# Last attention: VectorE's products for the weighted edges in pieces of 512 columns instead of 1024

## What is computed

```
h = (x @ W_att).reshape(n, H, D)                    # H = 8, D = 64
e = leaky_relu(a_src[src] + a_dst[dst], 0.2)
e = exp(e - segment_max(e, dst)[dst])
s = segment_sum(e, dst)
alpha = e / (s[dst] + 1e-16)
out = segment_sum(alpha[:, :, None] * h[src], dst)
att_out = out.mean(axis=1) + bias_att
```

## Time and profile before

| | |
|---|---|
| time, median of 3 runs | 5556.75 us (5547.52, 5556.75, 5561.84) |
| the profiled execution | 5550.81 us, of which its span is 5549.0 us |
| busy, whole span | DVE 73%, POOL 65%, PE 45%, ACT 23% |
| chain that ended last, by engine | POOL 52%, issue 20%, DVE 15%, PE 9% |
| chain that ended last, largest line | POOL, L789 (both attentions' gathers): 36% |
| gathers of the last attention (L789) | 864, from 4167.1 to 5300.7 us |
| L1848, whole run | 216 instructions of 1024 columns, 265.8 us |

### The profile page before, as it was taken

The page is one execution under the profiler, slowest core; times in us unless marked ns, Lnnn a source line. Parts: engine busy times, 40 slices in busy tenths (PEclk is TensorE's granted clock), DMA queues, the critical chain, the costliest instruction groups (busy, mean ns, idle before and its releaser), DMA issues.

```text
span 5549.0 us, 51316 instructions
## 1 busy us (share of the span) xinstructions
PE 2490.4 (45%) x13082; PEld 1703.0 (31%) x13082; DVE 4026.8 (73%) x7062; ACT 1267.1 (23%) x4430; POOL 3599.8 (65%) x3763
## 2 busy tenths in 40 slices
PE   1697100101121143423333344479864677677644
PEld 0571000001121132323232234457751233233224
DVE  9877888887886687878787878545543676776756
ACT  0000000000000011111111111110004777777741
POOL 2777777777777777777777777410017777777730
PEclk6555555555555555555555555589977888888876
DMA  6222111111222223232222223247741222222230
GB/s 250 56 55 57 48 55 48 55 61 51 53 52 71 54 80 82 80 82 80 81 81 82 78 76 98 73 152 255 236 126 46 79 91 78 79 87 82 76 101 13
DMA packets 392369, 477.20 MB, mean 86 GB/s; under 512 B 216403, under 2 KB 252309, under 8 KB 384966
## 3 DMA queue, kind: packets, MB, share of 16 engines
q1 hardware_dynamic: 136550, 279.94, 15.0%
q0 software_dynamic: 114832, 133.36, 10.5%
q10 hardware_dynamic: 140752, 61.28, 3.9%
HBM read 295.04 MB, written 179.24 MB: 85 GB/s over the span
## 4 chain that ended last, share of the span: by engine, by line
POOL 52%; issue 20%; DVE 15%; PE 9%; DMA 3%; ACT 0%; POOLq 0%; DVEq 0%; ACTq 0%; SPq 0%
POOL arena L789 36%; POOL rec_dram L746 13%; PE acc L2186 3%; DVE OHX L1515 3%; PE pw L2174 2%; DVE oh L1525 1%; DVE arena L1537 1%; DVE V L1557 1%; DVE arena L1541 1%; POOL own_dram L766 1%; DVE sc L1542 1%; PE acc L1993 1%; DVE oh L1515 1%; PE acc L2128 1%; POOL arena L819 1%
## 5 line engine op out<-in xcount | busy, mean ns | idle before, releaser
L789 POOL DMA_INDIRECT arena<-tab_dram,jst x2592 | 2521.5, 973 | 778.2 <-issue 773.0
L746 POOL DMA_INDIRECT rec_dram<-V,rowst x784 | 837.5, 1068 | 232.0 <-issue 225.3
L2120 PE MATMUL pw<-OHX 128*128 128x128 bf16 x1632 | 209.5, 309 | 789.7 <-DVE OHX L1515 788.4
L2128 PE MATMUL acc<-arena,oh 128*128 128x64 f32 x1952 | 428.6, 421 | 253.5 <-DVE oh L1525 253.5
L2128 PEld LDWEIGHTS acc<-arena,oh 128*128 128x128 f32 x1952 | 418.7, 331 | 267.8 <-issue 267.8
L970 ACT ACTIVATE arena<-arena,ew 128x64 f32<-128x64 f32 x1728 | 417.8, 333 | 34.4 <-PE acc L2220 34.4
L2220 PE MATMUL acc<-OHX,ident 128*128 128x512 f32 x432 | 254.7, 755 | 369.9 <-ACT OHX L970 369.9
L970 ACT ACTIVATE OHX<-arena,ew 128x64 f32<-128x64 f32 x1728 | 417.8, 333 | 2.5
L2120 PEld LDWEIGHTS pw<-OHX 128*128 128x128 bf16 x1632 | 156.0, 140 | 840.9 <-DVE OHX L1515 840.9
L1537 DVE TENSOR_TENSOR arena<-arena,pt 128x1024 f32<-128x1024 f32 x108 | 131.8, 1221 | 382.7 <-DMA arena<-tab_dram,jst 380.6
L739 POOL TENSOR_TENSOR pdum<-pdum 128x1 f32<-128x1 f32 x197 | 53.2, 270 | 449.7 <-DVE arena L1812 198.3
(11 more groups left out here) (566 smaller groups left out, 6244.8 us busy)
## 6 DMA issues: line engine op xcount, KB each, us to landing
arena<-tab_dram,jst POOLq DMA_INDIRECT x2592
arena<-rec_dram SPq DMA_DIRECT2D x122, 288.0 KB, 3.7
mt_dram<-oh ACTq DMA_DIRECT2D x272, 128.0 KB, 1.7
rows_dram<-V SPq DMA_DIRECT2D x27, 1056.0 KB, 4.0
rows_dram<-arena SPq DMA_DIRECT2D x27, 1056.0 KB, 4.3
V<-in_edge_attr_dram ACTq DMA_DIRECT2D x97, 256.0 KB
oh<-mt_dram SPq DMA_DIRECT2D x42, 512.0 KB, 4.7
OHX<-mt_dram SPq DMA_DIRECT2D x38, 512.0 KB, 4.7
```

Of the source, the lines that this page charges most:

```text
L746: gp.indirect_dma_start(rec[:, :], bass.IndirectOffsetOnAxis(ap=rowst[:, q, k:k + 1], axis=0), recst[:, q, k, :], None).then_inc(S[f"scat{ ...
L789: gp.indirect_dma_start(hd.G[:, a.r, j, :], None, table[:, :], row_of(jst[:, a.r, j:j + 1])).then_inc(S[f"rows{a.r}"], 16)
L2120: last = nc.tensor.matmul(unit_bank(c.slot)[:, k // 2 * P:(k // 2 + 1) * P], mones[c.slot][:, 0, k, :], mones[c.slot][:, 1, k, :], start=k ...
L2128: last = nc.tensor.matmul(o, roh[:, c.q, k, :], RG[:, c.r, k, 0:D], start=False, stop=True, skip_group_check=True)
```

## The change

VectorE's products of a step are made one edge at a time: four instructions of 512 columns instead of two of 1024, with the same inputs, outputs and places. Each of the first three raises the chain's semaphore and is waited for, where before only the first one was. The count of steps in a block's chain goes from 22 to 30 (2 more in each of 4 steps). Nothing else is changed: no DMA, buffer or other engine's instruction is added or moved.

```diff
             def weighted3(a, f, st):
 
                 slot_taken3(v, a, f)
-                for k in range(0, 8 - VA, 2):
+                for k in range(8 - VA):
                     t = f * 8 + k
-                    ins = V.tensor_tensor(V3r[vslot[f]][:, k * 512:(k + 2) * 512].rearrange("p (k h d) -> p k h d", h=H3, d=D),
-                                          G3[:, a.r, t:t + 2, 0:D].unsqueeze(2).to_broadcast([P, 2, H3, D]),
-                                          ew[:, a.q, t * H3:(t + 2) * H3].rearrange("p (k h) -> p k h", h=H3).unsqueeze(3)
-                                          .to_broadcast([P, 2, H3, D]), ALU.mult)
-                    if k + 2 < 8 - VA:
+                    ins = V.tensor_tensor(V3r[vslot[f]][:, k * 512:(k + 1) * 512].rearrange("p (h d) -> p h d", d=D),
+                                          G3[:, a.r, t, 0:D].unsqueeze(1).to_broadcast([P, H3, D]),
+                                          ew[:, a.q, t * H3:(t + 1) * H3].unsqueeze(2).to_broadcast([P, H3, D]), ALU.mult)
+                    if k + 1 < 8 - VA:
                         st(ins)
                     else:
                         ins.then_inc(S["dvd"], 1)
 
             def block3(a, c):
 
                 if a:
-                    st = Steps(v, "dc", 22, a.g)
+                    st = Steps(v, "dc", 30, a.g)
...
-                assert not a or st.k == 22, st.k
+                assert not a or st.k == 30, st.k
```

## The result

The changed kernel takes 5577.3 us (median of 5 runs, 5576.0 to 5581.2); the kernel before took 5555.2 in five runs beside them (5547.5 to 5561.8). The ratio is 1.0044, with a 95% interval from 1.0029 to 1.0058: slower by 22 us. Predicted were 5577 us, and slower. The profiled execution of the changed kernel took 5581.2 us, 5579.4 of it span.

A forecast was written before the change was run, and what follows sets the result against it. The last attention's time was taken as the sum of POOL's gathers. Added waits, 16 x 1.05 - 5 x 0.1 + 5 x 1.2 = +22 us, taken as 23, on a 5554 us base gave 5577 us; range 5562 to 5590.

The forecast's parts named there:

- POOL sets the stage: Last attention: its time is the sum of 864 gathers, 868.8 us busy, 53.2 of them waiting on VectorE's instructions.
- Length of a piece: L1848 with 512 columns: 0.692 us, taken from L1944's same shape; half a 1024-column instruction, 0.613, was the lower bound.
- Cover: VectorE's added 1.5 us a block costs nothing, hidden by waits on TensorE (2.3 us) and ahead of L1865 (9.0).
- The sum: Added gather waits over 26 blocks of the last attention: +22 us, 23 carried gather by gather.
- 16 common blocks: Gather blocks beside VectorE work like its block 13: each waits +1.05 us more.
- five first of a loop turn: Blocks where VectorE stands 0.43 us later ahead of its first products: waits change by -0.1 us each.
- five at the ends: Blocks at the two ends, whose first three product groups each meet a gather already: +1.2 us each.
- step 3: A block's last products, started by TensorE at any phase against gathers: waits 0.44 to 0.38 us, taken as 0.
- Rival 1: Gathers let through miss the next piece, so L1848's 43 us of waits become 22: 5533 us, chance 0.06.
- Rival 2: Gathers meet all product groups at any phase and L1831's waits stay: -4 us, 5550 us, chance 0.10.
- Rival 3: Idle time ahead of L1865 is gone, so VectorE's added work costs 42 us: 5596 us, chance 0.03.
- Rival 4: Each piece could stand 0.94 us behind a gather on the shared port: +165 us, 5719 us, chance 0.01.

The follow-up runs named there:

- runs 1: Kernel before, pairs kept, with a 352-column fill of an unused tensor on VectorE behind the products of a block's first three steps: 5593.9 us, stage 1171.7.
- run 7: Kernel before, VectorE's product pairs replaced by constant fills of 1024 columns that read nothing: 5568.8 us, stage 1150.4 where 1116 was expected.
- run 5: Changed kernel, but a piece does not wait for the one ahead of it: 5538.0 us, stage 1129.4.
- run 9: Changed kernel, pieces and waits kept, with a single-element sum ahead of the products of a block's first three steps: 5551.8 us, stage 1136.1.

## Why the prediction was right, step by step

- *POOL sets the stage, and a wait inside a gather moves all that follows.* Held: busy of L789 +24.4, stage +24.5, tail unchanged. In every run the stage is 1080.5 us and the waiting, within 0.2: 161.5 of waiting gave 1242.2, 22.6 gave 1103.0. Of the ten stages that were forecast ahead of their runs with a number, eight came within some 6 us; runs 1 and 7 missed by 16 and 34, both with a fill that starts late.
- *Length of a piece, 0.692 taken between 0.613 and 0.692.* Measured 0.693. The row of another line with the same shape was the right one to take. A piece and its wait took 0.726, as worked out.
- *Cover.* Held as named: steps 0 to 2 in the wait on TensorE, the rest ahead of the scores. The idle time there did not shrink by 1.5 us a block as the prediction's bound allowed, it grew by 0.6.
- *The sum.* Forecast were +1.05, -0.1 and +1.2 us for a block of each kind. Counted over all: 16 common blocks +1.17, five first of a loop turn +0.06, five at the ends +1.05; 18.7 + 0.3 + 5.3 = 24.3 us, against 22 by hand and 23 by replay. For the common block, term by term (measured: the 15 behind the first, which by themselves gained 1.20):

| | forecast | measured |
|---|---|---|
| step 0 | 0 to 0.28 | 0 to 0.28 |
| step 1 | 0.86 to 0.63 | 0.87 to 0.67 |
| L1831 behind it | 0.05 to 0.77 | 0.05 to 0.78 |
| step 2 | 0 to 0.28 | 0 to 0.28 |
| step 3 | 0.44 to 0.38, taken as 0 | 0.40 to 0.51 |

- *Where terms were off.* In the first blocks of a loop turn step 1 was to fall from 1.01 to 0.28, and step 2 to rise to 0.28; they came to 0.68 and 0.12. Two errors, +0.40 and -0.16, and step 3 fell there by 0.10; five blocks of 27 made them small. The step that failed is that VectorE stands 0.43 us later there. It did before, and not after: step 0 began 9.49 us behind the start of the scores before (9.05 to 9.08 in all common blocks but one), and 9.14 after. The time went from the idle stretch ahead of the first L1834, in the timeline before and after in the same block:

```profile
4886.94 0.69 DVE L1834 TENSOR_TENSOR V<-V,acc 128x512 f32<-128x512 f32 x1 [0.49 <-DVE V L1832]
```
```profile
4908.91 0.69 DVE L1834 TENSOR_TENSOR V<-V,acc 128x512 f32<-128x512 f32 x1
```

It is 0.49 us before and 0.13 after; why it got shorter stays open. Step 3, too, isn't at any phase, as the prediction had it: its wait goes by the block's place in the loop turn (before, from block 10 on: 0.94 to 0.97 us in the second, 0.27 to 0.41 in the third, 0.03 to 0.14 in the fourth). That the average over phases, 0.44, lies near their mean of 0.40 is luck. So it is partly luck, too, that the number came within 0.4 us of the median: the times of the kernel before alone lie between 5548.6 and 5555.2 over the four sets of runs.
- *By line.* The products went from 43.5 to 45.8 us while their waits more than tripled in number (58 to 195 of over 0.025 us, the longest 1.01 before and 0.50 now); L1831 went from 3.8 to 25.4. So almost all of the loss falls on an instruction that the change doesn't touch, as worked out. All waits of over 0.025 us were forecast at 310; there are 307.
- *Rival 1 (shorter instructions let gathers in sooner)* was right in that no wait is longer than 0.50, and wrong in that they are more: the products keep their sum. In run 5, where pieces follow each other faster, they do come to 22.9, near that rival's 22. *Rival 2 (phases don't stay)*: step 0 of each common block waits 0.27 to 0.28, block after block; they stay, and step 3's do too. *Rival 3 (VectorE the bound)*: 260 us idle ahead of the scores; and run 9 gives VectorE more to do and is faster than the change. *Rival 4 (VectorE held by whole gathers)*: a piece beside gathers grows by 0.004 us on average. "SBUF — State Buffer" of the Trainium skill, section "SBUF: two separate sides", lets whichever starts first block the other, where GpSimd reads SBUF (a gather reads its indices there); no run here shows that of a gather towards VectorE.

## What to carry to other kernels

Where one engine's small transfers or instructions set the time and another engine's instructions can hold them, count the collisions in the timeline before choosing the size of the other engine's instructions: here the same products went with 22.6 to 161.5 us of waiting in the stage, by the size, pace and phase of VectorE's instructions, and neither "shorter", "fewer" nor "without a wait" told the sign. In this kernel pace came first (pairs every 1.260 us beside gathers every 1.249 ran in step, every 1.144 did not), then the phase, which a tiny instruction of 0.17 us could set. Such a gain is bound to these very durations; it should be looked for again after every edit near it.

## What was not expected

- A constant fill on VectorE starts late: 0.10 to 0.13 us of idle time ahead of a small one, 0.28 or more ahead of a large one (run 7), where a product behind a product has 0.03. None of the 52 gathers that started inside one waited.
- Independent instructions without a wait between them overlap on VectorE in the trace: pieces of 0.69 start every 0.603 us, pairs of 1.225 every 1.144.
- The sum of a single element, 0.17 us three times a block, is worth 24 us of stage with pairs (1133.7 to 1110.1) and 22 with pieces (1158.2 to 1136.1).
